# Wave attention: the weights by tanh, one head at a time, and the value sums added in the output copy, for amplitudes up to one

## The reference, cut to what matters

```
FREQS = [31.0, 37.0, 41.0, 43.0, 47.0]
q, k, v = heads(x @ Wq.T + bq), heads(x @ Wk.T + bk), heads(x @ Wv.T + bv)
sim = einsum('bhid,bhjd->bhij', q, k) / sqrt(hd) / (abs(temperature)[0] + 0.1)
scores = zeros_like(sim)
for fi, freq in enumerate(FREQS):
    scores = scores + alpha[:, fi] * sin(TWO_PI * sim / freq + phi[:, fi])
w = sigmoid(scores)
w = w / (sum(w, axis=-1) + 1e-10)
out = einsum('bhij,bhjd->bhid', w, v)
```

```
'alpha': jax.random.normal(ks[5], (N_HEADS, len(FREQS))) * 0.1
factors = {..., 'L0_attn_a_alpha': 8.0, 'L0_attn_a_phi': 8.0, ...}
```

## Time and profile before

| | us |
|---|---|
| median of 3 runs | 3933.75 (3931.38 to 3935.47) |
| the profiled execution | 3933.19 |
| its span, first to last instruction | 3931.4 |
| VectorE busy | 2951.2 (75%) |
| ScalarE busy | 2817.8 (72%) |
| TensorE busy | 3171.9 (81%) |

### The profile page before, as it was taken

The page is one execution under the profiler, slowest core; times in us unless marked ns, Lnnn a source line. Parts: engine busy times, 40 slices in busy tenths (PEclk is TensorE's granted clock), DMA queues, the critical chain, the costliest instruction groups (busy, mean ns, idle before and its releaser), DMA issues. The chain is left out here.

```text
span 3931.4 us, 70146 instructions
## 1 busy us (share of the span) xinstructions
PE 3171.9 (81%) x26580; PEld 1974.0 (50%) x26580; DVE 2951.2 (75%) x4169; ACT 2817.8 (72%) x2401; POOL 925.5 (24%) x983
## 2 busy tenths in 40 slices
PE   4788888888888898898638943798998998998890
PEld 2232233223323332233236941688888888887790
DVE  7788888888888888888565545678787878876562
ACT  3999999999999999999604313576776776774330
POOL 2010111011010101110001442544334435330336
PEclk8899999999999999999868977799999999998995
DMA  5877887788788877877521225412213113112122
GB/s 160 306 295 301 301 330 293 303 311 320 299 306 317 309 300 299 333 293 297 220 71 63 62 54 171 68 27 36 47 20 54 27 27 56 26 18 71 33 61 69
DMA packets 311330, 683.35 MB, mean 174 GB/s; under 512 B 155296, under 2 KB 228608, under 8 KB 310560
## 3 DMA queue, kind: packets, MB, share of 16 engines
q1 hardware_dynamic: 302368, 661.87, 48.6%
q0 software_dynamic: 8704, 17.84, 2.0%
HBM read 90.73 MB, written 52.10 MB: 36 GB/s over the span
## 5 line engine op out<-in xcount | busy, mean ns | idle before, releaser
L740 PE MATMUL psA<-wave,diag 128*128 128x512 f32 x2560 | 1174.2, 606 | 117.3 <-DVE score L879 75.0
L801 ACT ACTIVATE wave<-wave 128x2048 f32<-128x2048 int32 x640 | 1184.8, 1904 | 45.6 <-DMA wave<-score 41.5
L740 PEld LDWEIGHTS psA<-wave,diag 128*128 128x128 f32 x2560 | 468.4, 191 | 727.5 <-issue 594.4
L879 DVE SCALAR_TENSOR_TENSOR score<-wave,par,psA 128x1024 f32<-128x1024 f32 x256 | 316.3, 1278 | 290.2 <-PE psA L740 290.2
L678 POOL TENSOR_TENSOR diag<-ident,par 128x128 f32<-128x128 f32 x384 | 142.5, 399 | 1493.5 <-PE psA L740 1493.3
L851 DVE TENSOR_SCALAR score<-s,par 128x2048 int32<-128x2048 int32 x384 | 482.1, 1285 | 9.2 <-DMA wave<-score 6.1
L879 DVE SCALAR_TENSOR_TENSOR score<-wave,par,score 128x1024 f32<-128x1024 f32 x384 | 470.3, 1282 | 0.0
L1785 POOL COPY kb<-ks 48x1024 bf16<-48x1024 bf16 x160 | 320.9, 2005 | 567.3 <-PE psR L1845 380.6
L716 PE MATMUL psO<-score,Vg 128*9 128x512 f32 x1056 | 284.6, 689 | 105.0 <-ACT score L781 105.0
L1935 ACT ACTIVATE W<-psR 128x1024 f32<-128x1024 f32 x256 | 249.4, 1023 | 133.3 <-PE psR L1870 133.2
L1926 ACT COPY r<-psR 128x1024 f32<-128x1024 f32 x256 | 248.6, 1021 | 103.9 <-PE psR L1845 103.9
(11 more groups left out here) (262 smaller groups left out, 4798.0 us busy)
## 6 DMA issues: line engine op xcount, KB each, us to landing
wave<-score SPq DMA_DIRECT2D x384, 1023.9 KB, 6.3
wave<-s SPq DMA_DIRECT2D x128, 1023.9 KB, 5.2
ks<-kb_parts SPq DMA_DIRECT2D x56, 384.0 KB, 6.2
qs<-qb_parts SPq DMA_DIRECT2D x32, 384.0 KB, 6.2
ys<-f_ys SPq DMA_DIRECT2D x36, 256.0 KB
wave_out<-og SPq DMA_DIRECT2D x33, 256.0 KB, 8.2
o<-wave_out SPq DMA_DIRECT2D x8, 1024.0 KB, 5.3
qp<-qa_parts SPq DMA_DIRECT2D x32, 192.0 KB, 7.2
```

The costliest lines, as they stand in the source:

```text
L740: mm = pe.matmul(psA[:, kt, :], diag[:, h % 2, f, :], wave[:, h % 2, f, kt * L:(kt + 1) * L], start=(f == 0), stop=(f == PE_F - 1 or (h in ...
L801: act.activation(wave[:, h % 2, f, :], angle[:, h % 2, f, :], ACT.Sin, scale=float(TWO_PI / 2.0 ** 32)).then_inc(sine, 1)
L879: return dve.scalar_tensor_tensor(out=score[:, u * HG + h, cols], in0=wave[:, h % 2, f, cols], scalar=par[:, u, 1, h * NF + f:h * NF + f + ...
```

## The change

ScalarE's weights move from four at a time, a group late, to one per head, two heads late (`weigh`). Where the flag is 0 they are Tanh of half the score in place of Sigmoid, and the output copy adds half of the column sum of the values and multiplies by 0.5; TensorE computes those sums (psV), VectorE halves them (`halve_values`). Where the flag is 1 they are Sigmoid and the copy is a plain copy, as before. Vg is padded to 32 columns a head and cleared once. `EVAC_HEADS` is empty, so the branches that test it never run and are cut here. The flag gets a second condition, the largest squared amplitude against NEAR.

```diff
+NEAR = 1.0
...
+    C_FIRST, C_VALUED, C_HALF, C_WEIGHED = 2, 4, 1, 2
+    C_ADDED, C_DIAG, C_TAKEN, C_STORED = 2 * HG * ADDS, 2 * HG, 2, 16
...
-        Vg = sb(c, "Vg", [P, 2, QT, HG, VW])
+        Vg = sb(c, "Vg", [P, 2, QT, HG, P // HG])
+        half_v = sb(c, "half_v", [P, 2])
+        reach = sb(c, "reach", [P, 1 + GPB * HG * NF])
+        top_reach = sb(c, "top_reach", [P, 1])
...
+            pool.memset(Vg[:], 0.0).then_inc(pads_clear, 1)
...
             def values(g, slot, heads):
                 if heads[0] == 0:
                     pe.wait_ge(v_ready, g + 1)
+                    pe.wait_ge(half_ready, g + C_HALF)
+                    for kt in range(QT):
+                        mm = pe.matmul(psV[:], Vg[:, slot ^ 1, kt, :, :].rearrange("p h d -> p (h d)"),
+                                       Vg[:, slot ^ 1, kt, 0, HD:VW], start=(kt == 0), stop=(kt == QT - 1))
+                    mm.then_inc(v_summed, 1)
                     pe.wait_ge(out_taken, g + C_TAKEN)
                 pe.wait_ge(weighed, g * HG + heads[-1] + 1)
...
-            def sigmoids(g, slot):
-                for h in range(HG):
-                    act.wait_ge(added, g * HG * ADDS - (HG - 1 - h) * ADDS + C_ADDED)
-                    act.activation(score[:, slot * HG + h, :], score[:, slot * HG + h, :], ACT.Sigmoid)\
-                       .then_inc(weighed, 1)
-
-            def outputs(g):
+            def weigh(m, at, general):
+                act.wait_ge(added, (m + 1) * ADDS + C_ADDED)
+                if general:
+                    act.activation(score[:, at, :], score[:, at, :], ACT.Sigmoid).then_inc(weighed, 1)
+                else:
+
+                    act.activation(score[:, at, :], score[:, at, :], ACT.Tanh, scale=0.5).then_inc(weighed, 1)
+
+            def outputs(g, slot, general):
 
                 act.wait_ge(valued, 2 * g + 2 + C_VALUED)
                 act.wait_ge(out_stored, g * 16 + C_STORED)
-                act.copy(og[:], psO[:]).then_inc(out_taken, 1)
+                if general:
+                    act.copy(og[:], psO[:]).then_inc(out_taken, 1)
+                else:
+
+                    act.wait_ge(half_ready, g + 1 + C_HALF)
+                    act.activation(og[:], psO[:], ACT.Identity, bias=half_v[:, 1 - slot:2 - slot],
+                                   scale=0.5).then_inc(out_taken, 1)
...
-                        if h == 0:
-                            sigmoids(g, 1 - u)
+                        weigh(n - 2, (u * HG + h - 2) % AR, general)
                         if h == HG - 1:
-                            outputs(g)
+                            outputs(g, 1 - u, general)
...
-                sigmoids(NG, 1)
-                outputs(NG)
-
+                for h in (HG - 2, HG - 1):
+                    weigh((NG - 1) * HG + h, HG + h, general)
+                outputs(NG, 1, general)
+
+            act.activation(og[:, 0:1], params[:, 0, 0, 0:1], ACT.Silu)
...
+            def halve_values(g, u):
+                dve.wait_ge(v_summed, g + 1)
+                dve.wait_ge(out_taken, g - 1 + C_TAKEN)
+                dve.tensor_scalar(half_v[:, u:u + 1], psV[:], 0.5, None, ALU.mult).then_inc(half_ready, 1)
...
                         add_sines(n, u, h, g)
-
-
-            dve.tensor_scalar(far[:], bound[:], FAR * min(FREQS) / HD, None, ALU.is_ge).then_inc(far_ready, 1)
+                        if h == 2:
+                            halve_values(g, u)
+
+
+            amps = params[:, :, 1, :]
+            dve.tensor_scalar(reach[:, 0:1], bound[:], HD / (FAR * min(FREQS)), None, ALU.mult).then_inc(reached, 1)
+            dve.tensor_tensor(reach[:, 1:].rearrange("p (a n) -> p a n", a=GPB), amps, amps, ALU.mult
+                              ).then_inc(reached, 1)
+            dve.wait_ge(reached, 2)
+            dve.tensor_reduce(top_reach[:], reach[:], AX.X, ALU.max).then_inc(reached, 1)
+            dve.wait_ge(reached, 3)
+            dve.tensor_scalar(far[:], top_reach[:], NEAR, None, ALU.is_ge).then_inc(far_ready, 1)
             dve.wait_ge(far_ready, 1)
```

More of the change, by code:

```diff
@@ L37 @@
 SPLIT_HEADS = (0, 1, 2, 3)
+EVAC_HEADS = ()
+NEAR = 1.0
 LEFT = "hhhmml"
@@ L552, in wave_attention @@
     C_SPS, C_SREADY, C_TURNED, C_CUT, C_SINE, C_USED, C_SUMMED = 2 * 2 * HG, 2, 2 * HG * (NF - 1), 2 * HG * NCUT, NF, 2 * PE_F, 4
-    C_FIRST, C_VALUED = 2, 4
-    C_ADDED, C_DIAG, C_TAKEN, C_STORED = 2 * HG * ADDS, 2 * HG, 1, 16
+    C_FIRST, C_VALUED, C_HALF, C_WEIGHED = 2, 4, 1, 2
+    C_ADDED, C_DIAG, C_TAKEN, C_STORED = 2 * HG * ADDS, 2 * HG, 2, 16
     with ExitStack() as c:
@@ L576, in wave_attention @@
         psO = ps(c, "psO", [P, L])
+        psV = ps(c, "psV", [P, 1])
         qk_loaded = [sem(c, f"qk_loaded{i}") for i in range(2)]
@@ L598, in wave_attention @@
         far_ready = sem(c, "far_ready")
+        v_summed = sem(c, "v_summed")
+        half_ready = sem(c, "half_v_ready")
+        pads_clear = sem(c, "pads_clear")
+        reached = sem(c, "reached")
         reduced = sem(c, "reduced")
@@ L662, in _ @@
         def _(pool):
+            pool.memset(Vg[:], 0.0).then_inc(pads_clear, 1)
             pool.tensor_copy(par[:, 0, :, :], params[:, 0, :, :]).then_inc(par_ready, 1)
+            pool.wait_ge(pads_clear, 1)
             with pool.Fori(0, B) as b:
@@ L670, in _ @@
                     pool.sem_inc(pool_step, 1)
-                    pool.tensor_copy(Vg[:, u, :, :, :], V[:, bass.ds(g, 1), :, :, :]
+                    pool.tensor_copy(Vg[:, u, :, :, 0:VW], V[:, bass.ds(g, 1), :, :, :]
                                      .rearrange("p a q h d -> p (a q) h d")).then_inc(v_ready, 1)
@@ L689, in _ @@
             pool.wait_ge(valued, 2 * NG - 2 + C_VALUED)
-            pool.tensor_copy(Vg[:, 0, :, :, :], V[:, NG, :, :, :]).then_inc(v_ready, 1)
+            pool.tensor_copy(Vg[:, 0, :, :, 0:VW], V[:, NG, :, :, :]).then_inc(v_ready, 1)
         @block.tensor
@@ L695, in _ @@
                               (used, C_USED), (summed, C_SUMMED), (added, C_ADDED), (diag_ready, C_DIAG),
-                              (out_taken, C_TAKEN),
+                              (out_taken, C_TAKEN), (half_ready, C_HALF),
+                              (weighed, C_WEIGHED),
                               (out_stored, C_STORED)):
@@ L716, in values @@
                         mm = pe.matmul(psO[row:row + VW, :],
-                                       Vg[:, slot ^ 1, kt, h, :],
+                                       Vg[:, slot ^ 1, kt, h, 0:VW],
                                        score[:, slot * HG + h, kt * L:(kt + 1) * L],
@@ L804, in pair @@
                                 tu, th, tg = (u, h + 2, g) if h < HG - 2 else (1 - u, h + 2 - HG, g + 1)
-                                take_scores(n + 2, tu, th, tg, f // 4, general)
-                        if h == 0:
-                            sigmoids(g, 1 - u)
+                                if f == 2 or th not in EVAC_HEADS:
+                                    take_scores(n + 2, tu, th, tg, f // 4, general)
+                        weigh(n - 2, (u * HG + h - 2) % AR, general)
                         if h == HG - 1:
-                            outputs(g)
+                            outputs(g, 1 - u, general)
             def all_heads(general):
                 for h in range(2):
-                    for half in range(2):
-                        take_scores(h, 0, h, 0, half, general)
+                    take_scores(h, 0, h, 0, 0, general)
+                    if h not in EVAC_HEADS:
+                        take_scores(h, 0, h, 0, 1, general)
                 act.wait_ge(cleared, 2)
@@ L852, in make_turns, with take_scores @@
                                   ALU.mult, ALU.add).then_inc(done, 1)
+            def take_scores(n, u, h, ng, general):
+                cols = slice(HALF, 2 * HALF)
+                dve.wait_ge(s_ps, n * 2 + 2 + C_SPS)
+                if not (isinstance(n, int) and n < 2):
+                    dve.wait_ge(carried[0][h % 2], (ng * (HG // 2) + h // 2) * 16)
+                if general:
+                    dve.tensor_copy(s[:, h % SR, cols], psS[:].rearrange("p a n -> p (a n)")).then_inc(s_ready, 1)
+                else:
+                    dve.wait_ge(par_ready, ng + 1)
+                    dve.tensor_scalar(first[:, h % SR, cols], psS[:].rearrange("p a n -> p (a n)"),
+                                      float(2 ** FRAC) / FREQS[0], par[:, u, 0, h * NF:h * NF + 1],
+                                      ALU.mult, ALU.add).then_inc(s_ready, 1)
             def make_angles(n, u, h, gn, general):
@@ L921, in pair @@
                             make_angles(n + 1, nu, nh, ng, general)
+                        tu, th, tg = (u, h + 2, g) if h < HG - 2 else (1 - u, h + 2 - HG, g + 1)
+                        if th in EVAC_HEADS and not (last and u == 1 and h >= HG - 2):
+                            take_scores(n + 2, tu, th, tg, general)
                         add_sines(n, u, h, g)
```

(8 more changed lines are left out.)

## The result

The changed kernel takes 7360.2 us (median of 4 runs, 7359.3 to 7367.4), where the runs of before beside it have a median of 3932.6. The ratio is 1.8725, 95% interval 1.8692 to 1.8757. Forecast were 7342 us, in a range of 7080 to 7560. The profiled execution took 7367.4 us, of which the span is 7365.7.

A forecast was written before the change was run, and what follows sets the result against it. ScalarE, with VectorE close behind, was taken to pace the wave attention. 3933.2 us plus 3408.3 (VectorE's loop 5236.6 against 1828.3) plus 0.8 for the flag's instructions gave 7342 us, range 7080 to 7560.

The forecast's parts named there:

- The flag: Largest squared amplitude 4.8 against NEAR 1.0, so the flag becomes 1 and every turn is reduced on VectorE first.
- The rival of 3831: Flag stays 0 and the tanh path runs, saving 80 table loads: 103 us less, 3831 us; chance 0.04.
- A, B, C, D: Per frequency on VectorE: A multiply and add ROUND, B subtract ROUND, C scalar_tensor_tensor, D conversion; 1.224, 1.224, 2.291, 1.285 us.
- Dependent starts: On VectorE, an instruction waiting for the one before starts 0.035 us after its end, 0.12 us dearer than independent.
- The rule of the Trainium skill: Every VectorE op drains before the next, semaphore or not, so the 15 waits a head are free: 7102 us, chance 0.08.
- The transfer wait: VectorE stands 3.5 us per head until the previous head's transfer 2 lands, 10.55 us after that head's angles end.
- The last head: At the loop's end, sines follow the transfers and two sums of 1.2 us close: 19.6 us after the angles' end.
- The loop: VectorE's wave loop: first head's angles 30.3, 127 periods of 40.84, last head 19.6; 5236.6 us against 1828.3.
- The angles of a head: Five frequencies on VectorE at 6.04 us each, 30.2 us a head.
- Edits costed at little: Flag's three VectorE instructions 0.8 us on the path; Sigmoid's table loads, value sums, halving and clearing of Vg all covered.

The follow-up runs named there:

- experiment 4: Changed kernel with the flag-1 branch's VectorE instructions interleaved for two frequencies: 7222.8 us; with transfers also asked for in order 1, 2, 3, 0: 6801.7 us.
- experiment 2: Changed kernel with SyncE asking for the transfers of frequencies 1, 2, 3, 0 in place of 0, 1, 2, 3: 6972.5 us.
- experiment 1: Two kernels: the changed one with NEAR = 100, flag 0, 3772.4 us; the kernel before with only the flag's new condition, 7373.7 us.
- e1_near: Changed kernel with NEAR = 100 in place of 1, so the flag is 0 and the tanh path runs: 3772.4 us, ratio 0.960.
- e8_near_no_silu: Changed kernel with NEAR = 100 and without the one Silu activation at the start of the wave stage: 4103.9 us, ratio 1.0495.
- e3_zero_last: Changed kernel with SyncE asking for the transfers of frequencies 1, 2, 3 and then 0: 6972.5 us.
- e9_long_loop: Changed kernel with transfers in order 1, 2, 3, 0 and VectorE's loop made of three pairs of groups an iteration: 6909.3 us, ratio 1.7678.
- e2_before_flag: Kernel before with nothing changed but the flag, which gets the condition on the amplitudes: 7373.7 us, ratio 1.874.
- e4_pairs: Changed kernel with the flag-1 branch's four VectorE instructions interleaved for two frequencies at a time (1 with 4, 2 with 3): 7222.8 us.
- e10_no_diag: Changed kernel with GpSimd's three 128x128 diagonal products per head left out, one single-column product standing in: 7300.3 us, ratio 1.8675.

## Why the prediction was right, step by step

- **The flag.** Right, and shown by both runs: 3772 us without its effect, 7374 with nothing else. The rival of 3831 for the path that doesn't run had the right sign and 59 us too little gain: it counted the loads and not what the spreading frees.
- **A, B, C, D.** Forecast 1.224, 1.224, 2.291, 1.285; measured 1.222 and 1.227 for the undisturbed A and B, 2.295, 1.292. That f32 runs at the speed of int32 in A, B and D held.
- **Dependent starts.** Forecast a gap of 0.035; the idle time of 13.2 us over 384 is 0.034. The rule of the Trainium skill, "VectorE: DVE Perf Modes", section "The DRAIN you can't avoid", was worth 240 us by the prediction's count, and the rows of small instructions were right against it; experiment 4 shows it at 2048 columns.
- **The transfer wait.** Forecast 3.5 us on 127 heads, about 445 us, measured 423.2, mean 3.33; transfer 2 lands 10.1 us after the angles' end, and 11.4 at the 14 jumps (10.55 forecast). Its cause, the order of release, is shown by experiment 2. The first wait lasts 9.3, as no sums stand before it; the sum by periods had that in it.
- **Not in the forecast.** GpSimd's products holding up A and B: 34 us. The jump back: about 2.0 us beyond the other waits, 14 times, in the 423.
- **The last head.** It lasts 23.4 us from its angles' end in place of 19.6. The forecast let two sums follow the fifth sine. In fact all five follow TensorE's sum psA, for which VectorE waits 10.2 us:

```profile
5363.54 2.47 DVE L927 SCALAR_TENSOR_TENSOR score<-wave,par,psA 128x1024 f32<-128x1024 f32 x2 [10.21 <-PE psA L758]
5365.93 3.67 DVE L927 SCALAR_TENSOR_TENSOR score<-wave,par,score 128x1024 f32<-128x1024 f32 x3
```

  That psA is late is in part the clock: the first six of this head's matmuls into psA start 0.86 us apart, at the lower of TensorE's two clock levels (1.2 and 2.4 GHz), the others 0.43. At the faster spacing the six would take 2.6 us less, an estimate from these starts. The mean granted clock is 0.67 in the stage and was 0.96 before. I had asked only whether TensorE's time fits into a head, and not what it does to the last head, beside which nothing else runs.
- **Together.** The loop was forecast at 5236.6 us and took 5263.0, 26.4 more. The angles of a head take 30.61 us on average and not 30.29, which is +41 over 128 heads, 34 of them GpSimd's doing; from their end to the next A it is 10.41 us and not 10.55, which is -18 over 127, jumps included; the last head gives +4. So every term but the last head's was right in kind, and the largest, the angles, within 1.1%; that the total came within 0.25% is in part luck, as the errors had different signs. The start was at 106.6, 0.8 us after the forecast one, and what follows is 2 us shorter.
- **Edits costed at little.** Right. ScalarE makes 256 loads in the stage and is busy for 2021 of its 5263 us; the value sums and the halving (0.15 us, 33 times) stand where nothing waits, and the flag alone costs as much as the whole change (experiment 1).

## What to carry to other kernels

Before the parts of a change are priced, find which branch they are in and work out the test on the inputs: here one comparison was worth 3440 us, and everything else in the diff 161, and that only where the comparison comes out the other way. A path that the program never took has the same terms as any other, and the rows of similar instructions elsewhere in the trace price it to about 1%; what they miss is what only shows when several engines run together. When two functions alternate on ScalarE, look for a table that holds both, and look in the trace whether it is used.

## What the runs showed of the hardware

- Sine and tanh alternate without a load when one Silu over one column stands ahead of them (e1_near); without it 256 loads stand in the stage, 1.28 us each, 357 us in all (e8_near_no_silu). No activation but Silu was tried.
- VectorE's loop of eight heads costs 2.9 us at each jump back in the long form (26 instructions on data and 15 waits on `reduced` per head, e3_zero_last: 40.5 us in 14 places), and nothing visible in the short one, where no idle time is put down to issue in front of L851. Four jumps in place of 14 took 32.5 us off (e9_long_loop). Where VectorE waits for a transfer anyway, the jump still adds 2.0 us (the changed kernel) or 3.1 (e2_before_flag, e4_pairs) to that wait.
- A VectorE instruction that waits for the one directly in front starts 0.035 us after its end; with another instruction between the two, and the same semaphore waits, it starts 0.08 to 0.09 before the end of the one in front (e4_pairs, 2048 columns).
- GpSimd's 128x128 product takes 1.60 us beside the general form and 0.40 in the kernel before (142.5 us for 384). VectorE's A beside it takes 1.42 us in place of 1.22 and B 1.30 in place of 1.23, while C isn't longer; without the products both are at 1.22 and 1.23 (e10_no_diag). The Trainium skill, "SBUF — State Buffer", section "Who interferes with whom", tells of a pair of ports that the two engines lock against each other for a whole instruction; that A and B are stretched agrees with it, and no run here separates the ports from another cause.
